# Turning the MLP input of a slot-attention kernel by VectorE's 32x32 blocks and SBUF moves in place of TensorE transposes

## The reference

```
k = ln(ctx) @ wk + bk ;  v = ln(ctx) @ wv + bv          # 1024 x 512 per batch
slots = q_mu + exp(q_logsig) * ln(x)                    # 1024 slots per batch
for _ in range(3):
    q = ln(slots) @ wq + bq
    attn = softmax over slots (k q^T * sqrt(512)) + 1e-8, normalised over the tokens
    slots = (attn^T v) @ wu + bu + slots
    h = ln(slots) @ w1 + b1
    slots = gelu(h) @ w2 + b2 + slots
    slots = ln(slots + cond)
x = x + slots
# then: score the tokens, route the best 256 of 1024 through attention and a gated MLP,
# and write them back over x + ln(x)
```

## Time and profile before

| | us |
|---|---|
| median of 3 runs | 2312.39 (2311.61 to 2317.55) |
| the profiled execution | 2315.96 |
| its span, first to last instruction | 2314.3 |
| TensorE busy in it | 2275.8 (98%) |
| VectorE busy | 1501.0 (65%) |
| ScalarE busy | 975.7 (42%) |
| GpSimd busy | 1000.7 (43%) |

### The profile page before, as it was taken

How to read it: one execution, slowest core, us unless ns; L and a number is a source line. 1 busy time by engine, 2 the same in 40 slices (tenths; PEclk the granted TensorE clock), 3 DMA queues, 4 the chain that set the end, 5 groups by cost and what they waited for, 6 DMA issues and landing times.

```text
span 2314.3 us, 30355 instructions
## 1 busy us (share of the span) xinstructions
PE 2275.8 (98%) x11317; PEld 1868.5 (81%) x11317; DVE 1501.0 (65%) x3056; ACT 975.7 (42%) x1650; POOL 1000.7 (43%) x1351
## 2 busy tenths in 40 slices
PE   8999999999999999999999999999999999999998
PEld 4788888888888888888888888888888887777886
DVE  6778557656476665769657576874766668764542
ACT  2566543343334333333333433333333345666432
POOL 3566235152453515435453452554535156653200
PEclk9999999999999999999999999999999999999999
DMA  5587000000152000013400001350000012204330
GB/s 202 181 315 283 3 1 1 1 1 1 37 208 79 1 23 5 15 50 128 155 6 21 8 10 55 113 170 5 10 19 1 21 55 81 74 29 146 97 113 19
DMA packets 87122, 158.54 MB, mean 69 GB/s; under 512 B 10801, under 2 KB 33337, under 8 KB 83134
## 3 DMA queue, kind: packets, MB, share of 16 engines
q1 hardware_dynamic: 82838, 150.26, 18.9%
q0 software_dynamic: 2688, 6.31, 0.9%
q10 hardware_dynamic: 1450, 0.04, 0.0%
HBM read 106.21 MB, written 50.37 MB: 68 GB/s over the span
## 4 chain that ended last, share of the span: by engine, by line
PE 81%; DVE 12%; POOL 2%; ACT 2%; issue 2%; DMA 0%; ACTq 0%; DVEq 0%; POOLq 0%
PE ps L218 25%; PE ps L220 25%; PE ps L219 25%; PE ps L1493 3%; DVE moments L1981 3%; DVE slots L2354 1%; DVE zTl L2029 1%; DVE tbuf L2341 1%; DVE tbuf L2348 1%; PE ps L444 1%; DVE mx L2303 1%; ACT prob L1885 1%; PE ps L1478 1%; PE ps L431 0%; PE ps L433 0%
## 5 line engine op out<-in xcount | busy, mean ns | idle before, releaser
L218 PE MATMUL ps<-zTh,kTl 128*128 128x512 f32 (+1 forms) x912 | 332.2, 364 | 2.9 <-ACT prob L1885 2.2
L220 PE MATMUL ps<-zTh,kTh 128*128 128x512 f32 (+1 forms) x912 | 324.6, 356 | 0.0
L219 PE MATMUL ps<-zTl,kTh 128*128 128x512 f32 (+1 forms) x912 | 324.3, 356 | 0.0
L218 PE MATMUL ps<-vh,prob_lo 128*128 128x512 f32 x768 | 304.6, 397 | 0.0
L220 PE MATMUL ps<-vh,prob_hi 128*128 128x512 f32 x768 | 299.9, 390 | 0.0
L219 PE MATMUL ps<-vl,prob_hi 128*128 128x512 f32 x768 | 299.2, 390 | 0.0
L2474 POOL TENSOR_SCALAR rs_m<-mv_m 128x1 f32<-128x1 f32 x96 | 60.2, 627 | 526.6 <-DVE mv_m L1983 526.6
L2029 DVE TENSOR_TENSOR zTl<-ps,zTh 128x512 fp32r<-128x512 f32 x224 | 151.0, 682 | 188.4 <-ACT zTh L1750 188.4
L1732 ACT ACTIVATE zbuf<-slots,rs_m 128x512 f32<-128x512 f32 x96 | 78.4, 816 | 333.7 <-POOL rs_m L2479 333.7
L1885 ACT ACTIVATE prob<-ps,nb 128x1024 f32<-128x1024 f32 x96 | 107.3, 1117 | 250.0 <-DVE nb L2308 246.0
L218 PEld LDWEIGHTS ps<-zTh,kTl 128*128 128x128 f32 x912 | 172.1, 189 | 35.1 <-DVE zTl L2029 7.1
(11 more groups left out here) (325 smaller groups left out, 5467.6 us busy)
## 6 DMA issues: line engine op xcount, KB each, us to landing
ctx<-in_ctx_dram SPq DMA_DIRECT2D x8, 1024.0 KB, 7.6
slots<-in_x_dram SPq DMA_DIRECT2D x8, 1024.0 KB, 6.7
kT_d<-kTh SPq DMA_DIRECT2D x6, 1024.0 KB, 8.1
kT_d<-kTl SPq DMA_DIRECT2D x6, 1024.0 KB, 10.6
s_d<-slots SPq DMA_DIRECT2D x6, 1024.0 KB, 5.2
v_d<-vh SPq DMA_DIRECT2D x6, 1024.0 KB, 9.2
v_d<-vl SPq DMA_DIRECT2D x6, 1024.0 KB, 11.2
kTh<-kT_d SPq DMA_DIRECT2D x3, 2048.0 KB, 11.0
```

Of the source, the lines that this page charges most:

```text
L218: nc.tensor.matmul(out, ll, rh, start=start, stop=False)
L219: nc.tensor.matmul(out, lh, rl, start=False, stop=False)
L220: return nc.tensor.matmul(out, lh, rh, start=False, stop=stop)
```

## The change

Seven of the eight MLP tiles of a round (`MOVED` = 7) are no longer turned by TensorE. VectorE turns the 16 blocks of 32x32 of each 128x128 square in place (`m_turn`), into the room of the probabilities that are used up; then SyncE moves the four bands of 32 partitions with four DMAs from SBUF to SBUF (`move`), so that band k of rows lies on all 128 partitions. The high and low parts are then taken from SBUF. After this a partition holds dimensions in mixed order, and all that meets it follows: `w1`, the query weight, three columns (`gq`, `gm`, `bm`), the query tiles and the eighth tile, whose normalise writes with a stride (`normalize_mixed`) and which TensorE still transposes. The orders of the engines in the update part are rewritten around it.

```diff
+    def blocks(j):
+        return prob[:, j // 4, 0:4, cut(j % 4)]
+    def moved(j):
+        return prob[:, j // 4, 4:8, cut(j % 4)]
+    MOVED = NT - 1
...
+            def load_mixed(k, done):
+                rows_ = a[k].rearrange("(g c i) n -> c i g n", g=4, c=C)
+                for c in range(C):
+                    sp.dma_start(wst[k][:, c, :], rows_[c]).then_inc(sem(done), 16)
...
+            def move(g, j):
+                sp.wait_ge(sem("tr_m"), g * NT + j + 1)
+                done, n = moved_in(g, j)
+                if n > 4 * 16:
+                    sp.wait_ge(sem(done), n - 4 * 16)
+                for k in range(4):
+                    sp.dma_start(moved(j)[:, k, :], blocks(j)[cut(k, 32)]).then_inc(sem(done), 16)
...
-                m_transpose(0); update(3); m_transpose(1); update(4); m_transpose(2); update(5)
-                m_transpose(3); update(6); m_transpose(4)
+                update(3); update(4); update(5); update(6)
...
-                m_transpose(5); update(7); m_transpose(6)
+                update(7)
...
             for k in COLS:
-                act.dma_start(cols[k][:, :], a[k]).then_inc(sem("cols_in"), 16)
+                src = a[k]
+                if k in ("gq", "gm", "bm"):
+                    src = src.rearrange("p c -> (p c)").rearrange("(c q) -> q c", c=C)
+                act.dma_start(cols[k][:, :], src, allow_slow_non_contiguous=k in ("gq", "gm", "bm"))\
+                    .then_inc(sem("cols_in"), 16)
...
+            for c in range(C):
+                if c == C // 2:
+                    act.wait_ge(sem("wst_b"), 2 * 16)
+                A.activation(wst["wq_mixed"][:, c, :].rearrange("p (c i g) -> p c i g", c=C, g=4), mixed(wst["wqT"][:, c, :]),
+                             ACT.Copy).then_inc(sem("wq_mixed"), 1)
...
+            def normalize_mixed(k, out, src, j):
+                return A.activation(out.rearrange("p (c i g) -> p g c i", c=C, g=4), src.rearrange("p (g c i) -> p g c i", g=4, c=C),
+                                    ACT.Identity, bias=rs[k][:, j, 1:2], scale=rs[k][:, j, 0:1])
...
                 def m_hi(j):
-                    hi_transposed("m", n8 + j, j, j)
+                    if j == MOVED:
+                        hi_transposed("m", n8 + j, j, j)
+                        return
+                    done, n = moved_in(g, j)
+                    act.wait_ge(sem(done), n)
+                    A.activation(zT[0][:, :, cut(j)].rearrange("p c (a n) -> p c a n", a=4),
+                                 moved(j).rearrange("p a (c n) -> p c a n", c=C), ACT.Copy).then_inc(sem("hi_m"), 1)
...
-            dve.wait_ge(sem("cols_in"), 16 * len(COLS))
+            dve.wait_ge(sem("cols_in"), 16 * (len(COLS) + 5))
...
+                def m_turn(j):
+                    dve.wait_ge(sem("zo_m"), n8 + j + 1)
+                    V.transpose(blocks(j), zbuf[:, j % 2, :].rearrange("p (g n) -> p g n", g=4)).then_inc(sem("tr_m"), 1)
...
+                    dve.wait_ge(sem("hi_m"), n8 + j + 1)
+                    V.tensor_tensor(zT[1][:, :, cut(j)].rearrange("p c (a n) -> p c a n", a=4),
+                                    moved(j).rearrange("p a (c n) -> p c a n", c=C),
+                                    zT[0][:, :, cut(j)].bitcast(f32).rearrange("p c (a n) -> p c a n", a=4),
+                                    ALU.subtract).then_inc(sem("lo_m"), 1)
...
+                m_turn(0)
                 add_update(1); finishes(9)
-                for j in range(4, NT - 1):
-                    add_update(j - 2); finishes(6 + j)
-                    split_prob(j)
-                    m_lo(j - 4)
+                split_prob(4)
+                m_turn(1); m_lo(0)
+                add_update(2); finishes(10)
...
```

More of the change, by code:

```diff
@@ L79, in build, with moved_in, mixed @@
     slots = at("slots", [P, NT, D], OP + 40 * KB)
+    def blocks(j):
[3 more added lines that the diff above has]
+    MOVED = NT - 1
+    def moved_in(g, j):
+        n = MOVED * g + j
+        return f"moved_in{n % 2}", (n // 2 + 1) * 4 * 16
+    def mixed(row):
+        return row.rearrange("p (g c i) -> p c i g", g=4, c=C)
     OR = OP + 56 * KB
@@ L148, in build @@
     wst["w2f"] = at("st_w2f", [P, C, D], 24 * KB)
+    wst["wq_mixed"] = at("st_wq_mixed", [P, C, D], 48 * KB)
     foldf = at("foldf", [P, D], 64 * KB)
@@ L1401, in _ @@
                     if t < ROUNDS - 1:
-                        finish_in(b - 1, t, 2, g); finish_out(b - 1, t, 2)
+                        finish_in(b - 1, t, 2, g)
                 if t < ROUNDS - 1:
+                    for j in range(MOVED):
+                        move(g, j)
+                        if b and j == 4:
+                            finish_out(b - 1, t, 2)
                     continue
@@ L1477, in fold @@
                         pe.wait_ge(sem("wst_b"), 2 * 16)
-                    last = nc.tensor.matmul(bank(fold_bank(u)), wst[wa][:, e, cut(t)], wst[wb][:, e, :],
+                    moving = wst[wb][:, e, :] if n else mixed(wst[wb][:, e, :])
+                    last = nc.tensor.matmul(bank(fold_bank(u)), wst[wa][:, e, cut(t)], moving,
                                             start=(e == 0), stop=(e == C - 1))
@@ L1483, in _ @@
             fold(0); fold(1)
[L1485 removed]
+            pe.wait_ge(sem("consts"), 4 + 2 * C)
             for k in range(2):
@@ L1525, in _ @@
             pe.wait_ge(sem("row_step"), C + 1)
-            col_product("wqT", kb, bank(1)[:, 0:4]).then_inc(sem("pcol"), 1)
+            pe.wait_ge(sem("wq_mixed"), C)
+            col_product("wq_mixed", kb, bank(1)[:, 0:4]).then_inc(sem("pcol"), 1)
             c_transpose(0, 2); c_transpose(0, 3)
@@ L1923, in slot_round @@
                 prob_split_hi(g, 2); prob_split_hi(g, 3)
-                for j in range(2, 6):
-                    if j >= 4:
-                        prob_split_hi(g, j)
-                        m_hi(j - 4)
-                    m_normalize(j - 2)
-                    finishes(6 + j)
-                prob_split_hi(g, 6); m_hi(2); m_normalize(4)
-                prob_split_hi(g, 7); m_hi(3); m_normalize(5)
-                m_normalize(6); m_hi(4)
-                for f in range(C):
-                    gelu(0, f)
-                m_hi(5)
-                m_normalize(7); m_hi(6)
-                m_hi(7)
+                m_normalize(0)
+                finishes(8)
+                prob_split_hi(g, 4); m_normalize(1); m_hi(0)
+                finishes(9)
+                prob_split_hi(g, 5); m_normalize(2); m_hi(1)
+                finishes(10)
+                prob_split_hi(g, 6); m_normalize(3); m_hi(2)
+                finishes(11)
+                prob_split_hi(g, 7); m_normalize(4); m_hi(3)
+                m_normalize(5); m_hi(4)
+                m_normalize(6); m_hi(5)
+                gelu(0, 0); gelu(0, 1); gelu(0, 2)
+                m_hi(6)
+                gelu(0, 3)
+                m_normalize(7); m_hi(7)
                 if last:
```

62 lines of the change are left out of this document (37 added, 25 removed).

## The result

| kernel | median, us | lowest to highest | runs |
|---|---|---|---|
| before | 2312.0 | 2311.6 to 2317.6 | 4 |
| after | 2359.3 | 2352.9 to 2368.1 | 4 |

The ratio is 1.0201, with a 95% interval of 1.0161 to 1.0242. The changed kernel is slower by 47 us. The forecast was 2335 us with a range of 2317 to 2359: the sign was right, the size was half of what came. The spread is news too: the kernel before repeats within 6 us, the changed one within 15.

What follows compares the result with a forecast made beforehand. TensorE, busy 98% of the span, was taken to bound the kernel. Nine rounds -1.6, three ranking rounds +16.2 and the start +7.9 gave +22.5 us, a median of 2335 us, range 2317 to 2359.

Runs made afterwards that it cites:

- all edits with the faulty order: Changed kernel plus turn behind next residual (ScalarE splits row 5 behind tile 2's normalise), contiguous fold operand, mixed columns last, key load behind moves: 2364.9 us.

## What to carry to other kernels

When work moves to an engine that has idle time, ask what it must wait for there, and who stands behind that wait: 2.3 us of idle time per tile were enough for 1.2 us of work, but not for a chain of 5 us ahead of it. Put the dependent work one iteration later and look at every engine's queue for the same mistake. And price a new pause of TensorE with the slower clock that may come behind it; in this kernel filling the twelve pauses with useless matmuls was worth 11 us.

## What was unexpected about the hardware

- Behind a pause of 2.98 us TensorE issued 128x512 matmuls every 0.43 us in place of 0.23 for some microseconds (granted clock 0.51). This came behind 10 of 12 pauses of 2.8 to 4.7 us in the changed kernel, and behind 4 of 12 of 2.98 us in the kernel before with one wait more. A fall there costs 1.3 to 2.9 us.
- Shorter waits can be followed by one too. The wait behind the twelfth round is 2.1 to 2.2 us long in all twelve profiled executions, and the clock falls at it or within 2.1 us behind it in seven. In the rounds a wait of 2.25 us was followed by none, one of 1.91 us (all edits with the faulty order, second round) by one, and those under 1.9 us by none.
- An fp32 matmul whose moving operand steps by 512 B took twice the time: 16 in 14.2 us against 7.0 contiguous.
- ScalarE's normalise of 128x512 with a write that steps by 16 B took 1.31 us against 0.82.
- VectorE's 32x32 block transpose of 128x512 fp32 took 0.71 us, where the low part, a subtraction of the same size, took 0.65.
